# One exponential per step for both heads of a step in an attention stage, with the row-score banks lent to the last block

## What is computed

```
Q = (query @ Wq).reshape(b, q_len, G, Hpg, dh)          # 16 heads: G = 4 groups of Hpg = 4, dh = 32
K = (key @ Wk).reshape(b, kv_len, G, dh)
V = (value @ Wv).reshape(b, kv_len, G, dh)
Q = Q / math.sqrt(dh)
scores = jnp.einsum('bqghd,bkgd->bghqk', Q, K) + m * rel   # ALiBi slopes
scores = jnp.where(mask[:, None, None, None, :], scores, neg)
w = jax.nn.softmax(scores, axis=-1)
out = jnp.einsum('bghqk,bkgd->bqghd', w, V)
out = out.reshape(b, q_len, G * Hpg * dh) @ Wo
```

## Time and profile before

| | us |
|---|---|
| three executions | 1182.73, 1189.04, 1196.71; median 1189.04 |
| span of the profiled execution, first to last instruction | 1146.9 |
| attention steps, first column score to the last one's step | 333.8 to 677 |
| PE busy in the whole span | 1028.8 (90%) |
| ACT busy in the whole span | 601.8 (52%) |

### The profile page before, as it was taken

How to read it: one execution, slowest core, us unless ns; L and a number is a source line. 1 busy time by engine, 2 the same in 40 slices (tenths; PEclk the granted TensorE clock), 3 DMA queues, 4 the chain that set the end, 5 groups by cost and what they waited for, 6 DMA issues and landing times. The chain is left out here.

```text
span 1146.9 us, 17729 instructions
## 1 busy us (share of the span) xinstructions
PE 1028.8 (90%) x5438; PEld 475.5 (41%) x5439; DVE 747.0 (65%) x1419; ACT 601.8 (52%) x898; POOL 456.0 (40%) x483
## 2 busy tenths in 40 slices
PE   0466889999789999999999998999998899999996
PEld 0243445555423223323322324455445455555542
DVE  6988988888786776578477547745545344443347
ACT  6897999999346776467467565452211111111110
POOL 1100335544410242243134341000657788889065
PEclk9978899999979999999999999998999899999998
DMA  9322930000534234134211004201678888976588
GB/s 325 114 74 80 342 138 1 2 1 9 133 89 107 80 82 116 62 58 94 66 48 44 12 21 136 76 26 52 243 282 170 200 205 207 206 192 146 153 284 291
DMA packets 174204, 142.39 MB, mean 124 GB/s; under 512 B 121364, under 2 KB 137108, under 8 KB 173624
## 3 DMA queue, kind: packets, MB, share of 16 engines
q1 hardware_dynamic: 163560, 110.40, 34.7%
q0 software_dynamic: 8672, 29.76, 7.9%
q10 hardware_dynamic: 1904, 1.38, 0.6%
HBM read 70.93 MB, written 43.37 MB: 100 GB/s over the span
## 5 line engine op out<-in xcount | busy, mean ns | idle before, releaser
L1432 ACT ACTIVATE prob<-p_col,mask_col,any_key 128x512 f32<-128x512 f32 x256 | 186.2, 781 | 103.2 <-PE p_col L1564 102.3
L1653 DVE CUSTOM_DVE_ANT_0 ajunk<-p_row,mask_row 128x512 bf16<-128x512 f32 x256 | 166.2, 686 | 64.1 <-PE p_row L1513 62.5
L1526 PE MATMUL p_out<-prob,v 128*64 128x512 f32 x512 | 138.1, 618 | 0.1
L1332 POOL TENSOR_TENSOR o<-sum_a,rec 32x512 f32<-32x512 f32 x30 | 39.1, 1304 | 186.1 <-DMA rec<-inv_d 184.0
L1513 PE MATMUL p_row<-ks,early_place 99*128 99x512 f16 x256 | 100.5, 395 | 8.7 <-DVE top L1653 8.0
L1564 PE MATMUL p_col<-early_place,ks 101*128 101x512 f16 x256 | 97.7, 385 | 0.9 <-ACT prob L1432 0.3
L2647 DVE SCALAR_TENSOR_TENSOR shid<-s_up,ssilu 128x352 f32<-128x352 f32 x39 | 20.4, 524 | 99.0 <-PE s_up L2565 98.8
L2513 ACT ACTIVATE ssilu<-s_gate 128x352 f32<-128x352 f32 x39 | 18.1, 463 | 124.0 <-PE s_gate L2565 124.0
L2578 PE MATMUL s_down<-mw,shT 128*128 (+1 forms) x351 | 82.0, 379 | 0.0
L2565 PE MATMUL s_gate<-mw,sxT 128*128 x444 | 74.1, 318 | 6.7 <-DMA sxT<-x_slots 6.7
L2565 PE MATMUL s_up<-mw,sxT 128*128 x444 | 73.5, 316 | 0.0
(11 more groups left out here) (354 smaller groups left out, 2077.3 us busy)
## 6 DMA issues: line engine op xcount, KB each, us to landing
x_slots<-nought SPq DMA_DIRECT2D x3, 3328.0 KB, 18.4
y_slots<-y SPq DMA_DIRECT2D x39, 256.0 KB, 2.2
early_place<-in_ctx SPq DMA_DIRECT2D x8, 1024.0 KB, 6.2
early_place<-halves_d SPq DMA_DIRECT2D x45, 128.0 KB, 2.5
halves_d<-halves SPq DMA_DIRECT2D x18, 256.0 KB, 2.1
mstg<-in_L_ffn_gate_w POOLq DMA_DIRECT2D x6, 704.0 KB, 5.7
mstg<-in_L_ffn_up_w POOLq DMA_DIRECT2D x6, 704.0 KB, 6.0
x<-in_x SPq DMA_DIRECT2D x4, 1024.0 KB, 7.3
```

What stands on the lines that cost most here:

```text
L1432: nc.scalar.activation(prob[s % 4][:, c, :], p_col[c][:], ACT.Exp, bias=mask_col[:, b, k:k + 1], scale=any_key[:, b:b + 1]).then_inc(t_exp, 1)
L1526: mm = nc.tensor.matmul(p_out[pr][c * 2 * DH:(c + 1) * 2 * DH, :], v1[b % 2][:, k, g, :], prob[n % 4][:, c, :], start=(k == 0), stop=(k == ...
L1653: nc.vector.tensor_tensor_reduce(junk[:, n % 2, :], p_row[n % 2][:], mask_row[:, blk // HPG, :], 1.0, -3e38, ALU.add, ALU.max, top[blk % 2 ...
```

## The change

The two banks `p_col` become one tensor of two banks, and so do the two banks `p_row`. ACT's two activations of 128x512 in a step become one of 128x1024, which waits for both column scores; `t_exp` counts one for each step. PE waits before the first column score of a step until the activation of the step before has ended, and no longer between the two. From step 121 (`FREE_ROWS`) every other step puts its column scores into the row scores' two banks, once all 256 maxima are done, and from there a step waits only for the exponentials of two steps before.

```diff
--- before.py
+++ after.py
@@ -1092,8 +1092,9 @@
     inv_d = nc.dram_tensor("inv_d", (2, GROUPS, S), F32).ap()
     halves_d = nc.dram_tensor("halves_d", (2, P, 2, S), F16).ap()
 
-    p_row = [ps(st, f"p_row{n}", [P, S], F32) for n in range(2)]
-    p_col = [ps(st, f"p_col{n}", [P, S], F32) for n in range(2)]
+    rows_bank = ps(st, "p_row", [P, 2, S], F32)
+    p_row = [rows_bank[:, n, :] for n in range(2)]
+    p_col = ps(st, "p_col", [P, 2, S], F32)
     p_out = [ps(st, f"p_out{n}", [P, S], F32) for n in range(2)]
     p_fill = [ps(st, f"p_fill{n}", [P, S], F32) for n in range(2)]
 
@@ -1110,6 +1111,12 @@
     BLOCK = 2 * KB
     STEPS = HPG * BLOCK
     BLOCKS = B * HPG
+    FREE_ROWS = (BLOCKS - 1) * BLOCK + 1
+
+    def col_banks(n):
+
+        return rows_bank if n >= FREE_ROWS and (n - FREE_ROWS) % 2 == 0 else p_col
+
     LATE = ("q", "k")
 
     ROWS_AT = (2,) * BLOCK
@@ -1424,13 +1431,11 @@
                     j, inb = divmod(s, BLOCK)
                     k = inb % KB
                     blk = HPG * b + j
-                    for c in range(2):
-                        n = 2 * (STEPS * b + s) + c
-                        if c == 0:
-                            need(act, t_pv, STEPS * b + s - 3)
-                        act.wait_ge(t_col, n + 1)
-                        nc.scalar.activation(prob[s % 4][:, c, :], p_col[c][:], ACT.Exp, bias=mask_col[:, b, k:k + 1],
-                                             scale=any_key[:, b:b + 1]).then_inc(t_exp, 1)
+                    n = STEPS * b + s
+                    need(act, t_pv, n - 3)
+                    act.wait_ge(t_col, 2 * (n + 1))
+                    nc.scalar.activation(prob[s % 4][:], col_banks(n)[:], ACT.Exp, bias=mask_col[:, b, k:k + 1],
+                                         scale=any_key[:, b:b + 1]).then_inc(t_exp, 1)
                     if inb == 1 and blk:
                         take_out(blk - 1, 1)
                     if inb == KB + 1:
@@ -1517,7 +1522,7 @@
                 blk, inb = divmod(n, BLOCK)
                 b = blk // HPG
                 pr, k = divmod(inb, KB)
-                pe.wait_ge(t_exp, 2 * (n + 1))
+                pe.wait_ge(t_exp, n + 1)
                 if k == 0:
                     need(pe, (t_outa, t_outb)[pr], blk)
                     if inb == 0 and blk % HPG == 0:
@@ -1560,8 +1565,13 @@
                     if inb == 0:
                         pe.wait_ge(t_tops, 64 * (blk + 1))
                     for c, g in enumerate(PAIRS[pr]):
-                        need(pe, t_exp, 2 * (STEPS * b + s) + c - 1)
-                        nc.tensor.matmul(p_col[c][:], ks[b % 2][0:ROWS_C, g, k * P:(k + 1) * P], qs[0:ROWS_C, j, g, :],
+                        n = STEPS * b + s
+                        if c == 0:
+                            if n == FREE_ROWS:
+                                pe.wait_ge(t_max, HEADS * BLOCKS)
+                            else:
+                                need(pe, t_exp, n - 1 if n > FREE_ROWS else n)
+                        nc.tensor.matmul(col_banks(n)[:, c, :], ks[b % 2][0:ROWS_C, g, k * P:(k + 1) * P], qs[0:ROWS_C, j, g, :],
                                          start=True, stop=True).then_inc(t_col, 1)
                         next_rows(1)
                     if s + b:
```

## The result

| | before | after |
|---|---|---|
| median of six executions, us | 1182.87 | 1194.90 |
| ratio, 95% interval | | 1.0082 [1.0045, 1.0120] |
| span of the profiled execution | 1146.9 | 1204.1 |
| from the first column score to the first matmul of the next stage | 357.57 | 369.76 |
| plain steps (52), mean | 1.982 | 2.195 |

The changed kernel is slower by 0.8% by the ratio, with an interval of 5.3 to 14.2 us; the two medians lie 12.0 us apart. In the two profiles the attention is 12.2 us longer. The spans differ by 57 us, and of this 44.7 lie behind the attention (455.6 against 500.3 us), in code that is the same in both; what that is comes with the experiments.

The account below looks back on a forecast made before the run. PE's own instruction stream was taken to set the attention's pace. 10.9 + 1.8 + 0.3 + 0.6 = +13.6 us on 1189.0 gave 1202.6 us, with range 1191 to 1213 (main case 1197 to 1208).

Parts of the forecast that it names:

- plain steps: Attention steps with row scores and no fill: 52 standing free go from 1.98 to 2.19 us, +10.9 us.
- the fixed points: Parts of a step: between column scores 0.44, to activation start 0.48, activation 1.21, back to PE 0.06; sum 2.19 us.
- 12-matmul steps: Attention steps where PE has a fill of 12 matmuls: it hides the wait, so they stay at 4.58 us.
- D: Rival: PE's new gaps lower its clock in a tenth of the stage, another 32 us, 1235 us; chance 0.05.
- C: Rival: the two banks take as long as two activations, 1.45 us; about +27 us, 1216 us; chance 0.08.
- B: Rival: PE's wait for the activation is hidden after all, about +1 us, 1190 us; chance 0.20.
- 1189.0 + 13.6: Forecast total: level before (profiled span 1146.9 plus 42.1 up to the median) plus the change's cost, 1202.6 us.
- the runs: 24 attention steps in runs ending in waits for DVE or ACT: lateness mostly hides the chain; +1.8 us, bounds 0 and 5.0.
- The side terms: Attention outside the 52 free steps: late runs +1.8, three top steps +0.3, last 12 steps +0.6 us.
- Three top steps: Steps with four transpositions, no fill, where ACT also casts and copies: next exponential about 0.1 late each, together +0.3 us.
- The last 12 steps: Attention's end, without row scores: first slower, then 1.55 us a step with two buffers, later end; +0.6 us, bounds -1 and +2.
- A: Main case: PE waits for the merged activation in the attention, +13.6 us, 1202.6 us, range 1197 to 1208; chance 0.63.

Follow-up runs that it names:

- with the check: Run-time bounds check on the expert's index in the last stage, added to the kernels before and after: medians 1144.23 and 1158.63 us, attention 357.21 and 369.16 us.
- two row scores between: Changed kernel with both row scores of a step between its two column scores instead of one: attention 388.48 us, plain step 2.411 us, one run.
- the two later ratios: Changed kernel plus a bounds check on the expert's index, run on two chips, against the kernel before without it: 1.0080 and 1.0111.

## Why the prediction was right or wrong

**Right: the mechanism and the main term.** Plain steps at 2.19 were forecast, 2.194 came, the fixed points (0.44, 0.48, 1.21, 0.06) each within 0.01, and 52 such steps gave +11.1 us (forecast +10.9). Fills hid the chain: 12-matmul steps stayed at 4.57 to 4.59. The clock did not fall (D; 1.00 in both stretches above), the activation took 1.21 and not 1.45 us (C), the wait was not hidden (B). Lengthening and shortening the chain moved the steps as its sum says, in both directions, so this is shown and not only argued.

**Wrong: two terms of the sum, the level of before and the side terms.** The mechanism held; the steps that failed are the 1189.0 of "1189.0 + 13.6" and, in the 13.6, the runs with their "what is late stays late".

**The level of before.** The six executions have a median of 1182.87, 6.2 us under the three that were shown, and of the 7.7 us between 1202.6 and 1194.9 this is the greater part. The other 1.6 us are the change itself, 12.0 for 13.6. The "42.1 us that lie between the span and the median" are no constant of the kernel either: an execution lasts 1.9 us longer than its span (1206.0 against 1204.1), so the profiled execution of before took about 1149 us, which is what this kernel takes on the faster chips. The forecast of the span, 1160.5, can therefore only be held against a profile from such a chip: 1157.5, with the check.

**The side terms: +2.7 forecast, +1.2 measured.** All three were off. "The runs" were put at +1.8 and gave +0.6 (50.7 to 51.3 us; 50.2 to 51.2 in the kernels with the check). The first two steps of the stage, which wait for DVE, took 9.27 us in every kernel but one (9.84 with two row scores between). The step of the prediction that failed here is "in most of them what is late stays late": in steps 33 to 35 the chain alone counts, 6.55 us in all three profiles of the changed kernel, 3 x 2.19, while before it was 6.77 and 6.23. DVE's lateness lies under the activation now. What is late on ACT does add to the chain (steps 26 and 58, 2.59 us). "Three top steps" at +0.3: two of them did take 2.30 and 2.31, but a late one before had taken more (2.52, now 2.22), and all 11 together came out 0.1 shorter. "The last 12 steps" at +0.6: +1.0, as the fast steps moved the wait to POOL's branch; it was named as "0.1 later still", and that wait grew from 0.74 to 1.65 us (with the check, from 0.52 to 1.26). The fill steps, for which nothing was put down, were 0.3 shorter; one of them, step 110, was late before (4.87 against 4.59). Together 11.1 + 0.6 - 0.1 + 1.0 - 0.3 is the 12.2 us, within rounding.

**The chances.** Slower by over 1% had 0.55, with the border at 11.9 us and the forecast at 13.6. The ratio of 1.0082 lies within 1%, which had 0.41. With 12 us in the medians and in the attention this was a matter of chance: the two later ratios, 1.0080 and 1.0111, fall on either side of 1%. The direction and the range 1191 to 1213 held; A's own range, 1197 to 1208, did not, as 1194.9 lies below it.

## What to carry to other kernels

Before merging two instructions that share a double buffer between them, write down the closed chain: start of the first producer to start of the consumer, the consumer's length, back to the producer. Merging saved 0.24 us of the consumer's time and moved its start back by 0.45. That is free only as long as the chain stays below the producer's own work; if it does not, move the other work of the producer (here the row scores) behind the last input. That took one line and gave 11 of the 12 us back. An engine that idles because it waits for the bottleneck has no time to be saved: 23 us taken from ACT by another edit shortened the attention by 0.7 us.

## What the runs showed of the hardware

A per-partition scale costs an exponential 91 to 92 ns, at 512 and at 1,024 columns alike: that of 512 takes 781 ns with it and 690 without, that of 1,024 takes 1206 and 1114. The border between two PSUM banks costs nothing that shows: the second bank adds 425 ns to an exponential (781 to 1206), and a copy of 1,024 f16 columns, which lie in one bank, takes 417 more than one of 512 f32 columns (1008 and 591 in the earlier trace rows). The attention, made of steps tied by semaphores, repeats to 0.2% between executions and chips, while the medians of the kernel before on two chips lay 3% apart (1147.32 and 1184.05 us).
